# A two-layer graph network on one core: the query products between the two sweeps move out of the chunk loop into a loop of their own behind it

## The reference

```python
x = _layernorm(x + _L0_gnn_ref(x, edge_index, L0_gnn_weight, L0_gnn_bias), axis=-1)
x = _layernorm(x + _L1_gnn_ref(x, edge_attr_64, edge_attr_32, edge_weight, src, dst, ...), axis=-1)
...
# layer 0
msgs = norm[:, None] * h[src]
out = jax.ops.segment_sum(msgs, dst, num_segments=num_nodes) + bias
...
# layer 1
w_ij = _mlp(edge_feats, rad_w0, rad_b0, rad_w1, rad_b1)
w_ij = w_ij + _mlp(chi_scalar, sph_w0, sph_b0, sph_w1, sph_b1)
q = (node_feats @ wq).reshape(-1, H, HD)[receivers]
k = (node_feats @ wk).reshape(-1, H, HD)[senders]
alpha = (q * w_ij * k).sum(axis=-1) / jnp.sqrt(jnp.float32(HD))
alpha = alpha * cutoffs[:, None]
v = (node_feats @ wv).reshape(-1, H, HD)[senders]
out = jax.ops.segment_sum(alpha[..., None] * v, receivers, num_segments=n_nodes) / AVG_NUM_NEIGHBORS
```

## Time and profile before

| | |
|---|---|
| median of 3 runs | 1785.33 us (1782.15 to 1786.39) |
| profiled execution | 1787.87 us, of which the profile's span is 1786.1 us |
| busy share of the span | PE 88%, DVE 78%, POOL 72%, ACT 52% |
| sweep 1 ends, stage between the sweeps begins | 635.7 us |
| first gather of sweep 2 | 679.48 us |
| last gather of sweep 2 | 1751.40 us |

### The profile page before, as it was taken

How to read it: one execution, slowest core, us unless ns; L and a number is a source line. 1 busy time by engine, 2 the same in 40 slices (tenths; PEclk the granted TensorE clock), 3 DMA queues, 4 the chain that set the end, 5 groups by cost and what they waited for, 6 DMA issues and landing times.

```text
span 1786.1 us, 45640 instructions
## 1 busy us (share of the span) xinstructions
PE 1572.9 (88%) x12982; PEld 1460.7 (82%) x12982; DVE 1384.6 (78%) x3866; ACT 921.6 (52%) x1393; POOL 1291.7 (72%) x1260
## 2 busy tenths in 40 slices
PE   3359999999989986999999999999999999999995
PEld 2248888888878875998988898889989989989994
DVE  8887776777777655788778787877887787878886
ACT  0055554455555465555555555555555555555553
POOL 6757777777777715777777777777777777777771
PEclk9999999999999988999999999999999999999997
DMA  3033333333333346666666666666666666666764
GB/s 99 13 106 105 108 100 100 99 107 103 100 109 100 94 134 164 183 186 178 170 174 174 178 173 171 173 176 174 178 182 171 173 175 179 177 170 174 187 183 106
DMA packets 177667, 259.30 MB, mean 145 GB/s; under 512 B 80699, under 2 KB 91765, under 8 KB 177444
## 3 DMA queue, kind: packets, MB, share of 16 engines
q0 software_dynamic: 51840, 132.72, 27.7%
q1 hardware_dynamic: 120016, 120.99, 24.0%
q10 hardware_dynamic: 5716, 4.55, 0.8%
HBM read 235.32 MB, written 22.79 MB: 145 GB/s over the span
## 4 chain that ended last, share of the span: by engine, by line
POOL 45%; issue 18%; DVE 15%; PE 11%; DMA 3%; DVEq 3%; POOLq 1%; SPq 1%; ACT 1%; ACTq 0%
POOL arena L699 43%; PE bank L1023 4%; DVE count L1368 4%; PE bank L980 4%; DVE xsplit L1335 2%; DVE key_hot L1356 2%; DVE low_hot L1355 2%; POOL tile_f L634 1%; DMA late<-in_dst_row 1%; DVE arena L1215 1%; PE bank L990 1%; DVEq L1341 1%; DMA arena<-kv_d,idx 1%; POOLq L716 1%; DVEq L1368 1%
## 5 line engine op out<-in xcount | busy, mean ns | idle before, releaser
L699 POOL DMA_INDIRECT arena<-kv_d,idx x808 | 826.9, 1023 | 264.4 <-issue 262.6
L980 PEld LDWEIGHTS bank<-w,hid 128*128 128x128 f32 x6464 | 788.9, 195 | 21.3
L980 PE MATMUL bank<-w,hid 128*128 128x128 f32 x6464 | 797.2, 279 | 0.0
L803 ACT ACTIVATE hid<-bank,b 128x512 f32<-128x512 f32 x808 | 495.3, 682 | 314.6 <-PE bank L964 296.2
L699 POOL DMA_INDIRECT arena<-xs_d,idx x408 | 395.7, 970 | 138.5 <-issue 132.0
L962 PE MATMUL bank<-xsplit,w_hi 128*128 128x512 f32 x808 | 344.9, 438 | 80.9 <-ACT hid L803 52.2
L795 ACT ACTIVATE xsplit<-xraw 64x1024 fp32r<-64x1024 f32 x202 | 212.3, 1052 | 230.6 <-DMA xraw<-in_sph_t 212.6
L1335 DVE TENSOR_TENSOR xsplit<-xraw,xsplit 64x256 fp32r<-64x256 f32 x808 | 288.0, 414 | 7.1 <-ACT xsplit L795 0.8
L962 PEld LDWEIGHTS bank<-xsplit,w_hi 128*128 128x128 f32 x808 | 154.8, 192 | 114.6 <-ACT hid L803 60.7
L1368 DVE TENSOR_TENSOR count<-count,bank 128x200 f32 x400 | 144.8, 362 | 123.5 <-issue 58.3
L990 PE MATMUL bank<-onehot,late 128*128 128x126 f32 x1616 | 215.6, 282 | 6.2 <-DVE late L1544 4.4
(11 more groups left out here) (147 smaller groups left out, 1290.8 us busy)
## 6 DMA issues: line engine op xcount, KB each, us to landing
late<-relrow_d SPq DMA_DIRECT2D x103, 256.0 KB
xraw<-in_rad_t SPq DMA_DIRECT2D x205, 128.0 KB
xraw<-in_sph_t SPq DMA_DIRECT2D x410, 64.0 KB
w_sb<-w_d SPq DMA_DIRECT2D x52, 256.0 KB, 3.9
w_d<-w_sb SPq DMA_DIRECT2D x51, 256.0 KB
arena<-kv_d,idx POOLq DMA_INDIRECT x808
arena<-xs_d,idx POOLq DMA_INDIRECT x408
qwin<-q_d SPq DMA_DIRECT2D x101, 31.5 KB
```

The lines of the kernel that those rows point to most:

```text
L699: pool.indirect_dma_start(gath[:, k, t * width:(t + 1) * width], None, table, bass.IndirectOffsetOnAxis(ap=idx[:, pair.slot(4), j * TILES ...
L803: act.activation(hid[:, s.slot(2), c, :], hid_ps[s.sub(4, c, 4 * s.total).slot(len(hid_ps))][:, :], ACT.Silu, bias=b0[:, c:c + 1]).then_in ...
L980: mm = pe.matmul(w_ps[:, t * D:(t + 1) * D], hid[:, b, c, t * P:(t + 1) * P], w1[:, c, :], start=False, stop=(c == 3), skip_group_check=True)
```

## The change

Keys and values of all seven chunks come first. The queries' products (PE), both roundings (ACT), both differences (DVE) and the stores of the parts (SP) stand in a loop of their own behind it on each of these engines. For that the transposed chunks, of which two were kept, are all kept (`x_t` grows from 1024 to 3200 columns), `q_rest` gets two buffers in the place of `prod` (which sweep 2 uses later), and DVE and ACT take the steps of two chunks in turn. The number of instructions of each kind stays.

```diff
-        x_t, to = part(count, 0, 2 * CHUNK * P)
-        x_t = x_t.rearrange("p (k f) -> p k f", k=2)
-        q_rest, to = part(count, to, CHUNK * D)
+        x_t, to = part(count, 0, NB * P)
+        q_rest = prod
...
# SP
                 sp.dma_start(kv_d[rows, :].rearrange("(b p) f -> p b f", p=P),
                              kv_out[:, c % 4, 0:n, :]).then_inc(s_kvt[c % 4], 16)
+
+            for c in range(CHUNKS):
+                n, rows = len(blocks(c)), slice(blocks(c)[0] * P, (blocks(c)[-1] + 1) * P)
                 sp.wait_ge(s_lo, c + 1)
...
# ACT
                 act.wait_ge(s_tr, c + 1)
-                if c >= 2:
-                    act.wait_ge(s_proj, blocks(c - 2)[-1] + 1)
...
             for c in range(CHUNKS + 1):
                 if c < CHUNKS:
                     copy_transposes(c)
-                if c >= 1:
-                    q_hi(c - 1)
                 if c + 1 < CHUNKS:
                     scaled(c + 1, s_shift, s_norm)
                 if c >= 1:
                     copy_kv(c - 1)
-                    q_mid(c - 1)
                 if c + 2 < CHUNKS:
                     root(c + 2, s_var, s_std)
+            for c in range(CHUNKS + 1):
+                if c < CHUNKS:
+                    q_hi(c)
+                if c >= 1:
+                    q_mid(c - 1)
...
# PE
-                    project(c - 1)
-            project(CHUNKS - 1)
+                    project_kv(c - 1)
+            project_kv(CHUNKS - 1)
+            for c in range(CHUNKS):
+                project_q(c)
             pe.wait_ge(s_projc, (NB + 1) // 2)
+            pe.wait_ge(s_rest, CHUNKS)
...
# DVE
-                if c >= 1:
-                    split_q(c - 1)
+            for c in range(CHUNKS + 1):
+                if c < CHUNKS:
+                    rest_of_q(c)
+                if c >= 1:
+                    low_of_q(c - 1)
```

More of the change, by code:

```diff
@@ L855, in copy_transposes @@
                 act.wait_ge(s_tr, c + 1)
-                if c >= 2:
-                    act.wait_ge(s_proj, blocks(c - 2)[-1] + 1)
                 cols = slice(0, len(blocks(c)) * P)
-                act.activation(x_t[:, c % 2, cols], bank[2 + c % 2][:, cols], ACT.Copy).then_inc(s_trc, 1)
+                own = slice(blocks(c)[0] * P, (blocks(c)[-1] + 1) * P)
+                act.activation(x_t[:, own], bank[2 + c % 2][:, cols], ACT.Copy).then_inc(s_trc, 1)
             def q_hi(c):
@@ L870, in q_mid @@
                 act.wait_ge(s_rest, c + 1)
-                act.activation(q_parts[:, c % 4, 1, cols], q_rest[:, cols], ACT.Copy).then_inc(s_mid, 1)
+                act.activation(q_parts[:, c % 4, 1, cols], q_rest[:, c % 2, cols], ACT.Copy).then_inc(s_mid, 1)
             def copy_kv(c):
@@ L1075, in transpose, with project_kv, project_q @@
                 mm.then_inc(s_tr, 1)
-            def project(c):
+            def project_kv(c):
                 pe.wait_ge(s_trc, c + 1)
+                for b in blocks(c):
+                    if b >= 4 and b % 2 == 0:
+                        pe.wait_ge(s_projc, b // 2 - 1)
+                    to = b % 2 * 2 * D
+                    pe.matmul(bank[6 + b // 2 % 2][:, to:to + 2 * D], x_t[:, b * P:(b + 1) * P], wqkv[:, D:3 * D],
+                              start=True, stop=True, skip_group_check=True).then_inc(s_proj, 1)
+            def project_q(c):
                 if c >= 2:
@@ L1082, in project @@
                     at = b % CHUNK * P
-                    mm = pe.matmul(bank[4 + c % 2][:, at:at + D], x_t[:, c % 2, at:at + P], wqkv[:, 0:D],
+                    mm = pe.matmul(bank[4 + c % 2][:, at:at + D], x_t[:, b * P:(b + 1) * P], wqkv[:, 0:D],
                                    start=True, stop=True, skip_group_check=True)
                 mm.then_inc(s_projq, 1)
[L1086 to L1091, removed]
             convolve(0)
@@ L1462, in scale_and_shift, with rest_of_q, low_of_q @@
                                          op0=ALU.mult, op1=ALU.mult).then_inc(s_shift, 1)
-            def split_q(c):
+            def rest_of_q(c):
                 cols = slice(0, len(blocks(c)) * D)
                 dve.wait_ge(s_hi, c + 1)
-                if c >= 1:
-                    dve.wait_ge(s_lo, c)
-                dve.tensor_tensor(q_rest[:, cols], bank[4 + c % 2][:, cols], q_parts[:, c % 4, 0, cols],
+                if c >= 2:
+                    dve.wait_ge(s_lo, c - 1)
+                dve.tensor_tensor(q_rest[:, c % 2, cols], bank[4 + c % 2][:, cols], q_parts[:, c % 4, 0, cols],
                                   ALU.subtract).then_inc(s_rest, 1)
+            def low_of_q(c):
+                cols = slice(0, len(blocks(c)) * D)
                 dve.wait_ge(s_mid, c + 1)
-                dve.tensor_tensor(q_parts[:, c % 4, 2, cols], q_rest[:, cols], q_parts[:, c % 4, 1, cols],
+                dve.tensor_tensor(q_parts[:, c % 4, 2, cols], q_rest[:, c % 2, cols], q_parts[:, c % 4, 1, cols],
                                   ALU.subtract).then_inc(s_lo, 1)
```

## The result

The changed kernel takes 1779.24 us (median of 15 runs, 1769.94 to 1785.37). The kernel before took 1782.55 us beside it (15 runs, 1776.61 to 1786.87). The ratio is 0.9969, 95% interval 0.9956 to 0.9983: it is faster, by about 5.5 us (0.0031 x 1785; the interval allows 3.0 to 7.9). The forecast said 10.0 us.

The account below looks back on a forecast made before the run. POOL's unbroken gathers were taken to bound sweep 2, so the end follows the first gather. 9.0 + 2.1 - 0.7 - 0.4 = 10.0 us, hence 1785.33 - 10.0 = 1775.3 us, range 1771 to 1782.

Parts of the forecast that it names:

- The bound: Sweep 2: POOL issues gathers without a break, 1071.9 us, and the end is the last gather plus 34.7 us.
- ACT and PE, 9.0 us: Stage between the sweeps: query work leaves ACT's queue, so the last copy of keys and values ends 9.0 us earlier.
- SP, 2.1 us: Stage's end: the last store of keys and values no longer stands behind query stores, gaining 2.1 us.
- First gather less last store is 3.71 us, which stays: Start of sweep 2: the time from issuing the last store of keys and values to the first gather stays 3.71 us.
- the prediction's 0.7: Stage between the sweeps: 0.7 us given back for one more slow PE product and last two stores following more closely.
- Gathers beside query work, 0.4 us: Start of sweep 2: the first eight gathers or so run beside DVE's differences and lose 0.4 us.
- The queries: After keys and values: the query loop ends later, so the first product of keys and queries starts at most 3 us later.
- the first rival: Sweep 2: consumers never catch up; 1785 to 1788 us, or 1791 if query stores take 5 us longer; chance 0.06.
- the gathers' upper cost: Rival at sweep 2's start: gathers run slower by 4.2 us instead of 0.4, giving 1779.1 us; chance 0.10.
- the second rival: "The gain is smaller than can be measured": PE at the lower clock for three chunks of keys and values; 1780.5 us; chance 0.09.
- as forecast: The main case for the whole kernel: likeliest 1775.3 us, range of its own 1772 to 1779; chance 0.75.
- The signs: Trace signs: first gather at 668 to 671, transposes' copies 3.3 to 3.8 us apart, sweep 2's gathers within 2 of 1071.9.

Follow-up runs that it names:

- Late gathers: Changed kernel with POOL clearing its accumulator three more times between the landing of keys and values and the first gather; ratio 1.0016, median 1786.88 us.
- doubled query stores: Changed kernel with the stores of query parts of chunks 3 to 6 issued a second time, into a spare tensor; ratio 0.9979, median 1783.69 us.
- late clearing: POOL clears its accumulator only after DVE's last statistics step of the stage; ratio 0.9939 in the changed kernel, 1.0000 in the kernel before.
- slower chips: Four runs, of the changed kernel and small edits, on two other chips where every kernel takes about 2510 us; ratios 0.9973 to 1.0009.
- 48 more stores: Changed kernel with the stores of query parts of chunks 3 to 6 issued four more times into a spare tensor; ratio 1.0105, median 1800.77 us.

## Why the prediction was right in its sign and too large in its size

**The bound: right.** POOL gathers without a break in sweep 2, and the end follows the first gather. Late gathers (gain gone) and doubled query stores (gain kept) show it from both sides.

**ACT and PE, 9.0 us: the step that failed.** It measured 5.2 (37.71 - 32.54). "PE sets a floor under that ... each holds the other a little; I take off 0.5" counted the work of PE and ACT in a chunk, and not that POOL's clearing of the accumulator holds DVE's variance step. The trace of before held both parts: the clearing, which the prediction used only for when POOL was free, and the variance step of 1.32 us, which is not among its rows. In the new order the step meets the clearing 0.75 us after its start (655.77 - 655.02), before it was 1.59 us, so it is held longer, 2.15 us.

With late clearing the last copy ends at 28.87 us (663.25 - 634.38), 8.8 before the kernel before's 37.71, where the sum had 9.0. **That the two agree so well is in part luck**, since these 8.8 us also contain the old collision, which the prediction took for the order's work. Of the 1.3 us that ACT waited for DVE's difference, 0.94 stood behind the clearing. Without the collision the old order's last copy ended at 35.3 us in two profiles and at 36.22 in a third. The third is the fair match, since PE's clock ran at its lower level early in the stage as long as with late clearing in the changed kernel. Against it the new order is worth 7.3 us, and 6.8 between two such profiles of the slower chips (36.22 and 29.43), not 9.0.

The changed kernel's loss against late clearing, 3.7 us at the last copy and 3.6 at the first gather, has two main parts. *The hold itself* was there in each execution of the new order with early clearing (2.12 to 2.15 us) and costs about its length. *PE's clock* is the other part. In two profiled executions (first gather at 37.23 and 37.44) the granted clock fell from 2.4 to 1.2 GHz beside chunk 4's product, after PE had waited for norms, and the product took 3.45 us instead of 1.97; an earlier stretch at the lower level, 6 us into the stage, was 6.8 us long. With the same hold, in the runs with 48 more stores, with late gathers and on the slower chip, the early stretch was 3.4 us long, the clock did not fall beside chunk 4, and keys and values were 2.4 us earlier, 0.8 of it from the early stretch.

The kernel before and the two runs that changed only its order of stores had all of it too: the long early stretch, the hold, and a slow product of chunk 4 (2.82, 3.33 and 2.76 us). In the six profiles with late clearing the clock never fell there, though four had the long early stretch. So in all fourteen profiles it fell where the long stretch and the hold came together, and nowhere else. Why, and what makes the early stretch long or short, is open. The prediction had set 0.7 aside for one more slow product and for stores that follow each other more closely; the product alone cost 1.5 where it came.

The Trainium skill (SBUF — State Buffer, Who interferes with whom) says that a DVE `tensor_scalar` can run in a mode that takes the port pair shared with GpSimd, and that whichever of the two comes second blocks until the first is done. The trace agrees: an instruction of 0.17 us was held and ended within 0.02 us of the memset's end, in both kernels (657.92 against 657.90, and 661.04 against 661.02). In which mode the step ran no trace shows. The prediction had weighed this section for the gathers only, and the place where such a hold counted was another.

**SP, 2.1 us: right.** The last store was issued 0.03 us after the last copy (667.51 against 667.48), which gives 2.3.

**"First gather less last store is 3.71 us, which stays": wrong.** It is 4.66, and 4.75 with late clearing. It stayed where the kernel before was kept and only SP's last stores were moved (3.51). Splitting a store made it 5.18. The last two stores are now issued 0.49 us apart (667.02 and 667.51), before 3.18 (672.59 and 675.77), and 0.96 in the run where it stayed 3.51. That is the likely reason, but only argued; the prediction's 0.7 was meant for it too. So the first gather's sum is 5.2 + 2.3 - 0.95 = 6.5 us, as measured.

**Gathers beside query work, 0.4 us: right.** The 15 gathers up to 691 us took 14.57 us, 0.97 each, 0.3 us more than 15 times 0.95. The upper end of 4.2 us, to which the rule of the Trainium skill (SBUF — State Buffer, Who interferes with whom) on two SBUF inputs pointed, did not come.

**The queries: right in kind, 3 us off.** The first product of keys and queries started at 691.55, forecast 686 to 689. The first store of a part was issued at 670.77 instead of 667, the last at 685.4 instead of 679 to 681. Some 3 us are those of the keys and values ahead. Beyond that ACT's first rounding waited for earlier stores to free the buffer (2.82 us in the chain above at 674.86), a wait between SP and ACT that "three stores in 1.42 us" left out. Gathers beside them also slow the stores, as the first rival had it: the stores of query parts took 3.3 us to land (median, 2.0 to 4.2), and 2.3 (2.0 to 3.0) in the run with late gathers. All this cost nothing: the first message was done at 698.64, 14 us before the ninth group was gathered (713.06), and the consumers caught up in nine bodies, forecast 6 to 10.

**The number.** 1775.3 was forecast; the changed kernel's gain of 5.5 us against a term sum of 10.0 is the first gather's 6.5 instead of 10.4. The time, 1779.24 us, lies in the stated range of 1771 to 1782, in which the gathers' upper cost and part of the second rival had been let in; it is just past the 1779 of "as forecast", and a gain of 0.31% stands at the edge of the rival "the gain is smaller than can be measured". That rival's mechanism, products of keys and values at the lower clock for three chunks, came late in the stage for one chunk, as it had before. The version with late clearing moves the first gather by 10.1 us and takes 10.9 us off (0.0061 x 1786; the interval allows 7.3 to 14.5).

**The signs.** POOL's 0.3 us, the last store right behind the last copy, the wait for queries and SP's shorter wait came as told. The first gather at 672.17 missed its 668 to 671, and the copies of transposes were 3.1 to 5.0 us apart instead of 3.3 to 3.8, the 5.0 behind the held step. First to last gather was to stay within 2 us of 1071.9 and came out 4.5 below; it scattered over 11.6 us in the profiles without a wait of POOL, so that sign was too narrow to tell anything, and the span's 11.1 us near the forecast's 10.0 is luck.

## What to carry to other kernels

When a stage is made shorter, look for every instruction that an idle engine runs beside it, not only at those that were moved: a clearing that nobody waited for held a 0.17 us step on the path for 2.15 us, and one more wait took it away. In the profile such a hold shows as a small instruction with ten times its usual duration that ends with another engine's. A delay of the consumers costs nothing as long as the ring isn't full and they have reserve; it is worth working out where that ends before the order is chosen, since behind this point the delay comes back. Of 26 us here 21 did, though the first message had been done 14 us ahead of its need.

## What the runs showed of the hardware that was not expected

- A DVE instruction of 128x4 elements was held by a POOL memset until that ended (2.12 to 2.15 us in the new order, 1.32 in the old), while DVE's statistics steps (L1440, L1443), which ran beside the first 0.7 us of the same memset, kept their usual 0.16 to 0.28 us.
- With the same program up to that point PE's clock fell in two profiled executions beside one product (3.43 and 3.45 us) and not in three others (1.97 us), one of them on a slower chip. In the two it had been at its lower level for 6.8 us early in the stage, in the three for 3.4.
- The whole kernel took about 1783 us on some chips and about 2510 on two others, with the stage between the sweeps as fast as elsewhere and both sweeps slower.
